# A recurrent layer stack in 279 steps: tile kinds grouped on TensorE, the residual added head by head, growth logarithms kept in the down bank

## The reference, cut to what matters

```python
for l in range(L):                                       # 4 layers
    x = x + _slstm_layer(_ln(x, ln1_w[l]), ...)          # convolution over 4 tokens, gates, recurrence, norm per head
    x = x + _ffn(_ln(x, ln2_w[l]), ff_up[l], ff_down[l]) # gelu(x@up_g) * (x@up_v) @ down, 256 -> 2*336 -> 256
...
def step(carry, wx_t):                                   # 256 steps in order, batch 32, 4 heads of 64
    h, c, n, m = carry
    raw = wx_t + jnp.einsum('bhd,hdgo->bhgo', h, rk) + b
    ir, fr, zr, og = (raw[:, :, 0], raw[:, :, 1], raw[:, :, 2], raw[:, :, 3])
    lfm = m + jax.nn.log_sigmoid(fr)
    mn = jnp.maximum(ir, lfm)
    ig = jnp.exp(ir - mn)
    fg = jnp.exp(lfm - mn)
    cn = fg * c + ig * jnp.tanh(zr)
    nn = fg * n + ig
    hn = jax.nn.sigmoid(og) * cn / nn
    return ((hn, cn, nn, mn), hn)
```

## Time and profile before

| | us |
|---|---|
| median of 3 runs | 3738.53 (3736.28 to 3739.94) |
| the profiled execution, its own time | 3732.63 |
| its span | 3730.9 |
| PE busy | 3615.0 (97%) |
| DVE busy | 3460.5 (93%) |
| ACT busy | 3064.7 (82%) |
| POOL busy | 2253.7 (60%) |

### The profile page before, as it was taken

One profiled execution on the slowest core, in us unless ns is written; L12 is line 12 of the kernel. 1 busy time (PEld: TensorE's weight loads), 2 busy tenths in 40 slices (PEclk: granted clock), 3 DMA queues, 4 the chain that ended last, 5 costly groups with the idle time before them and its releaser, 6 DMA issues. The chain is left out here.

```text
span 3730.9 us, 167466 instructions
## 1 busy us (share of the span) xinstructions
PE 3615.0 (97%) x71481; PEld 2282.1 (61%) x71481; DVE 3460.5 (93%) x9241; ACT 3064.7 (82%) x6357; POOL 2253.7 (60%) x2395
## 2 busy tenths in 40 slices
PE   6999999999999999999999987999999999999997
PEld 3666666665666666666666654666666666666664
DVE  8999999999999999999999987889988898888886
ACT  4999999999999999999999984677776677777675
POOL 3777777777777777777777764444444444444442
PEclk9999999999999999999999998999999999999998
DMA  2000221000000000000000000000000000100000
GB/s 82 25 25 25 56 59 53 25 25 25 25 25 25 25 25 25 25 25 25 25 25 25 25 26 18 24 24 24 24 24 24 24 24 28 32 24 24 24 16 10
DMA packets 99973, 104.27 MB, mean 28 GB/s; under 512 B 17297, under 2 KB 95005, under 8 KB 98729
## 3 DMA queue, kind: packets, MB, share of 16 engines
q1 hardware_dynamic: 99224, 93.56, 8.7%
HBM read 48.52 MB, written 17.53 MB: 18 GB/s over the span
## 5 line engine op out<-in xcount | busy, mean ns | idle before, releaser
L565 POOL TENSOR_TENSOR conv_products<-normed_features,conv_taps_by_token 128x256 f32<-128x256 f32 (+1 forms) x837 | 757.9, 919 | 530.2 <-ACT normed_features L348 530.1
L771 POOL TENSOR_TENSOR exps_of_both_halves<-scores 128x256 f32<-128x256 f32 x512 | 424.2, 851 | 583.8 <-ACT scores L1027 578.4
L295 PE MATMUL banks<-up_centred,after_cell_features 128*32 128x336 f32 x8928 | 740.3, 449 | 1.1 <-ACT after_cell_features L348 0.5
L295 PEld LDWEIGHTS banks<-up_centred,after_cell_features 128*32 128x32 f32 x8928 | 260.5, 109 | 277.6 <-issue 224.1
L302 PE MATMUL banks<-down,hidden_features 112*32 112x256 f32 x6696 | 419.2, 383 | 0.0
L578 POOL TENSOR_TENSOR conv_partial_sums<-conv_products,conv_partial_sums 128x512 f32<-128x512 f32 x279 | 370.5, 1328 | 21.9
L1027 ACT ACTIVATE scores<-scores 128x512 f32<-128x512 f32 x512 | 305.4, 626 | 77.7 <-DVE scores L1175 74.0
L366 ACT ACT_TABLE_LOAD x279 | 358.0, 1283 | 5.2
L381 ACT ACT_TABLE_LOAD x279 | 358.0, 1283 | 5.1
L1175 DVE SCALAR_TENSOR_TENSOR scores<-banks,score_top 128x512 f32<-128x512 f32 x512 | 327.9, 681 | 26.1 <-PE banks L857 25.5
L269 PE MATMUL banks<-recurrent_weights,h_features 64*32 64x256 f32 x8928 | 313.1, 379 | 0.3 <-DVE h_features L509 0.2
(11 more groups left out here) (222 smaller groups left out, 9933.3 us busy)
## 6 DMA issues: line engine op xcount, KB each, us to landing
layer_inputs<-layer_outputs SPq DMA_DIRECT2D x279, 96.0 KB, 2.0
layer_inputs<-in_x SPq DMA_DIRECT2D x280, 32.0 KB, 1.8
x_scratch<-layer_outputs SPq DMA_DIRECT2D x279, 32.0 KB
x_tokens<-in_x SPq DMA_DIRECT2D x32, 256.0 KB, 3.0
context_features<-in_ctx SPq DMA_DIRECT2D x32, 256.0 KB, 3.7
layers_out<-x_scratch SPq DMA_DIRECT2D x32, 256.0 KB, 2.8
out<-result SPq DMA_DIRECT2D x64, 128.0 KB, 1.8
up_centred<-in_ff_up SPq DMA_DIRECT2D x1, 2688.0 KB
```

What stands on the lines that cost most here:

```text
L295: mm = nc.tensor.matmul(bank[group(l), b, 0:UP], xmt[:, n, group(l)], up[:, l, n, at:at + UP], start=n == 0, stop=n == HALF - 1, skip_grou ...
L565: return nc.gpsimd.tensor_tensor(prod[:, i:i + n], xnt[:, j % NRING].rearrange("p n t -> p (n t)")[:, None, :].broadcast_to([P, n, HALF * ...
L771: nc.gpsimd.tensor_tensor(psum[:, i % RING, :], pr[:, i % RING, 0:S], pr[:, i % RING, S:2 * S], ALU.add).then_inc(halves_added, 1)
```

## The change

On PE the order of a step is new: all transposes stand together (`xm`, `xn`, `h`, `hid`), then all products of 64x32 tiles (convolved, recurrent, centred, the bias of the next step, its products of `xnt`), then down, then both up products. On ACT the tanh of z and o open the step, the copies of `ht` (formerly DVE's) and `xnt` stand behind the exponential of the growth, the copy of `xmt` between the exponential and the logarithm of f. The growth logarithm is written into the second half of the bank of the down product, not into the gates; the transposes of `hid` go into the old gate banks. On DVE `yn` is gone: four operations of 128x64, one per head, scale and add the residual at once. `dl` is made at the end of a step, right behind `sf`, and `h`'s second half stands ahead of `hid`. On POOL both 256-wide products come first, then the wide sum, the wide product, and the two other sums, all for the same token.

```diff
+    def hidden_of(j):
+        q = 2 * (j % 2)
+        return bank[0:UT, q:q + 2, :].rearrange("p r (n h t) -> p (r n) h t", n=HALF, h=2)[:, 0:UTILES, 1, :]
...
             for j in range(STEPS):
-                reach(pe, xm_done, j)
                 transposes(CV, D, xm[:, (j - 1) % MRING], xmt_ready)
                 transposes(CV, 0, xn, xnt_ready)
-                add_bias(j)
-                by_head(j, wg, xnt[:, (j - 1) % NRING], 2, GATES)
-                pe.wait_ge(xmt_copied, j + 1)
-                feed_up(UPG, 0).then_inc(g_done, 1)
                 pe.wait_ge(h_done, HALF * (j + 1))
                 transposes(FD, D, h, ht_ready)
-                pe.wait_ge(xnt_copied, j + 1)
-                hidden_features().then_inc(hidt_ready, 1)
+                pe.wait_ge(hid_done, j + 1)
+                hidden_features(j - 1).then_inc(hidt_ready, 1)
                 pe.wait_ge(xs_done, j + 1)
                 by_head(j, wg, xst, 0, 2)
                 pe.wait_ge(ht_copied, j + 1)
                 by_head(j, rk, ht, 0, GATES).then_inc(rec_done, 1)
                 centred().then_inc(cen_ready, 1)
+                pe.wait_ge(ls_done, j + 1)
+                add_bias(j + 1)
+                pe.wait_ge(xnt_copied, j + 1)
+                by_head(j + 1, wg, xnt[:, j % NRING], 2, GATES)
                 pe.wait_ge(hidt_copied, j + 1)
+                pe.wait_ge(grown, j + 1)
                 feed_down().then_inc(down_done, 1)
-                pe.wait_ge(yn_done, j + 1)
+                pe.wait_ge(xmt_copied, j + 1)
+                pe.wait_ge(xm_done, j + 1)
+                feed_up(UPG, 0).then_inc(g_done, 1)
                 feed_up(UPV, UP).then_inc(up_done, 1)
...
+                nc.scalar.activation(gate(j - 1, 2), gate(j - 1, 2), ACT.Tanh).then_inc(z_done, 1)
+                nc.scalar.activation(gate(j - 1, 3), gate(j - 1, 3), ACT.Tanh, scale=0.5).then_inc(o_done, 1)
+                reach(act, d_ready, j)
                 nc.scalar.activation(td[:], dl[:], ACT.Tanh, scale=-0.5).then_inc(td_done, 1)
...
-                copy(both(xmt[:]), bank[:, CV, D:]).then_inc(xmt_copied, 1)
-                copy(both(xnt[:, j % NRING]), bank[:, CV, 0:D]).then_inc(xnt_copied, 1)
...
+                act.wait_ge(ht_ready, j + 1)
+                copy(both(ht[:]), bank[:, FD, D:], 1.0 / H_SCALE).then_inc(ht_copied, 1)
+                copy(both(xnt[:, j % NRING]), bank[:, CV, 0:D]).then_inc(xnt_copied, 1)
                 act.wait_ge(growth_exp, j + 1)
-                act.wait_ge(h_done, HALF * (j + 1))
-                nc.scalar.activation(gate(j - 1, 1), heads(spb[:]), ACT.Ln, bias=1.0).then_inc(growth_log, 1)
+                act.wait_ge(ht_copied, j + 1)
+                nc.scalar.activation(bank[:, FD, D:], spb[:], ACT.Ln, bias=1.0).then_inc(growth_log, 1)
...
                 nc.scalar.activation(heads(fb[:]), gate(j, 1), ACT.Exp).then_inc(f_exp, 1)
+                copy(both(xmt[:]), bank[:, CV, D:]).then_inc(xmt_copied, 1)
                 act.wait_ge(f_exp, j + 1)
                 nc.scalar.activation(fb[:], fb[:], ACT.Ln, bias=1.0).then_inc(f_log, 1)
...
-                nc.vector.tensor_tensor(yn[:].rearrange("p (r n d) -> p r n d", r=2, n=HALF),
...
+                for r in range(2):
+                    for n in range(HALF):
+                        at = slice(r * P + n * DH, r * P + n * DH + DH)
+                        add = nc.vector.scalar_tensor_tensor(out=xm[:, j % MRING, at], in0=bank[:, UPG + r, UP + n * DH:UP + n * DH + DH],
+                                                             scalar=rs[:, 2 * n + r:2 * n + r + 1], in1=xr[:, (j - 3) % XRING, at],
+                                                             op0=ALU.mult, op1=ALU.add)
+                add.then_inc(xm_done, 1)
...
-                reach(pool, taps_rest, j)
-                nc.gpsimd.tensor_tensor(new[:, 3], prod[:, 3], new[:, 4], ALU.add).then_inc(sum3_done, 1)
                 reach(pool, xnt_copied, j)
                 reach(pool, conv_done, j)
+                products(0, 1, j - 1).then_inc(taps_first, 1)
                 products(1, 1, j - 1).then_inc(taps_second, 1)
-                products(0, 1, j - 1).then_inc(taps_first, 1)
-                pool.wait_ge(taps_first, j + 1)
                 reach(pool, sum2_done, j)
+                pool.wait_ge(taps_second, j + 1)
                 nc.gpsimd.tensor_tensor(new[:, 0:2], prod[:, 0:2], old[:, 1:3], ALU.add).then_inc(conv_done, 1)
+                products(2, 2, j - 1).then_inc(taps_rest, 1)
+                pool.wait_ge(taps_rest, j + 1)
+                nc.gpsimd.tensor_tensor(new[:, 3], prod[:, 3], new[:, 4], ALU.add).then_inc(sum3_done, 1)
                 nc.gpsimd.tensor_tensor(new[:, 2], prod[:, 2], old[:, 3], ALU.add).then_inc(sum2_done, 1)
-                pool.wait_ge(xnt_copied, j + 1)
-                pool.wait_ge(sum2_done, j + 1)
-                products(2, 2, j).then_inc(taps_rest, 1)
```

More of the change, by code:

```diff
@@ L346, in _, with copy @@
         def _(act):
-            def copy(dst, src):
-                return nc.scalar.activation(dst, src, ACT.Copy)
+            def copy(dst, src, scale=1.0):
+                return nc.scalar.activation(dst, src, ACT.Copy, scale=scale)
             def both(ap):
@@ L381, in _ @@
                 nc.scalar.preload_act_table(ACT.Gelu)
-                act.wait_ge(sf_done, j + 1)
-                nc.scalar.activation(gate(j, 3), gate(j, 3), ACT.Tanh, scale=0.5).then_inc(o_done, 1)
-                nc.scalar.activation(gate(j, 2), gate(j, 2), ACT.Tanh).then_inc(z_done, 1)
-            act.wait_ge(z_done, STEPS)
+            act.wait_ge(f_log, STEPS)
         @block.vector
@@ L390, in _ @@
             for buf, val in ((xr, 0.0), (h, 0.0), (half_r, 0.0), (ls, NEVER), (dl, 0.0), (xm, 0.0), (xst, 0.0), (prod, 0.0), (hid, 0.0),
-                             (hidt, 0.0), (xnt, 0.0), (xmt, 0.0), (gl, 0.0), (xn, 0.0), (v, 0.0), (sf, 0.0), (rstd, 0.0), (eps, EPS), (bias, 0.0), (pick16, 0.0),
+                             (hidt, 0.0), (xnt, 0.0), (xmt, 0.0), (gl, 0.0), (xn, 0.0), (stat2, 0.0), (rstd, 0.0), (eps, EPS), (bias, 0.0), (pick16, 0.0),
                              (mean_w, 1.0 / D), (begun, 0.25 * H_SCALE), (never, 0.0)):
@@ L399, in _ @@
                 n += 2
+            nc.vector.bn_stats(stat2[:], xm[:, 0]).then_inc(w_step, 1)
+            n += 1
             dve.wait_ge(w_step, n)
@@ L538, in _ @@
                                                op1=ALU.max).then_inc(sf_done, 1)
-                dve.wait_ge(yn_done, j + 1)
-                nc.vector.tensor_tensor(xm[:, j % MRING], yn[:], xr[:, (j - 3) % XRING, :], ALU.add).then_inc(xm_done, 1)
+                dve.wait_ge(sf_done, j + 1)
+                dve.wait_ge(v_done, j + 1)
+                nc.vector.scalar_tensor_tensor(out=dl[:], in0=v[:], scalar=-60.0, in1=sf[:], op0=ALU.max,
+                                               op1=ALU.subtract).then_inc(d_ready, 1)
                 dve.wait_ge(down_done, j + 1)
```

60 lines of the change are left out of this document (26 added, 34 removed).

## The result

The changed kernel takes 3807.64 us (median of 4 runs, 3805.31 to 3809.13), the kernel before 3737.69 on the same chip (4 runs). The ratio is 1.0186, with a 95% interval of 1.0168 to 1.0204: 70 us slower. The forecast was 3760, with 3684 to 3791 as its range. The direction was right and the size was not.

A forecast was written before the change was run, and what follows sets the result against it. PE was taken to set the 7.75 us step, ACT close behind. After the change the loop of POOL's wide product, `dl` and ACT, 4.38 + 3.45 = 7.83, adds 22 us over 279 steps to 3738.5: 3760, range 3684 to 3791.

The forecast's parts named there:

- The loop of the wide product, `dl` and ACT: `dl` ends 0.28 after POOL's wide product, ACT then copies `xnt`: 4.38 + 3.45 = 7.83 us a step, 22 us more; chance 0.64.
- the spacings of "0.30" and their neighbours: Three unknown ACT spacings in the loop, to tanh, gelu and exponential, each put at 0.30 us, between 0.28 and 0.32.
- 7.73 to 7.94: Range of the loop's step in us, from three spacings of 0.28 to 0.32 and one of 0 to 0.09.
- PE alone would need 7.42: Grouping PE's products by tile kind saves 0.33 us a step, leaving PE 7.42 of its own.
- the seven and in the four: PE's changes of tile kind a step, seven before and four after, at 0.11 us each.
- not 0.7 to 0.8: Sign in the changed profile: the `dl` row on VectorE grows from 0.49 to 0.7 or 0.8 us.
- The recurrence at 7.58: Path of the recurrence through all engines, a sum of spacings: 7.58 us a step, below the loop's 7.83.
- `dl` does meet POOL: Against the free-port rival: `dl` meets no POOL instruction, the recurrence decides at 7.58, 47 us less, 3691; chance 0.22.
- restart whole: Rival: `dl` restarts whole after POOL's instruction, 0.13 us more a step, 7.96, total 3797 us; chance 0.05.
- misses its gap: Rival: `xn` comes after POOL's wide sum has begun, 1.03 us more a step, some 4050 us; chance 0.04.
- faster: Outcome faster than before, by the free port or PE's own pace (3646 to 3671 us): chance 0.24.
- slower: Outcome slower than before, by the rest of the loop's case and the two rivals above it: chance 0.66.

The follow-up runs named there:

- e14: Changed kernel with `sf` written into the PSUM bank of the transposes, and PE's bias and normed products of the next step behind both up products: 3684.4 us, ratio 0.9853.
- e9: Changed kernel with `sf` in the PSUM bank and PE's down products between the centred products and the next step's bias: 3734.8 us, ratio 0.9997.
- e1: Changed kernel, but POOL's wide product waits until `dl` has ended: 3749.3 us, ratio 1.0039.
- e3: Changed kernel, but POOL's wide product of 128x512 is split into two products of 128x256 in the same place: 3751.0 us, ratio 1.0038.
- e8: Changed kernel with POOL's order untouched, but `sf` written into the PSUM bank of the transposes, so `dl` reads one operand from PSUM: 3739.0 us, ratio 1.0009.
- e5: One of the nine kernels with runs of 96 short products; the text does not tell what it changed or its time.
- e4: Kernel before with only POOL's loop taken from the changed kernel: 3809.5 us, ratio 1.0204.
- e7: Changed kernel with POOL's order of before put back: 3847.7 us, ratio 1.0291.

## Why the prediction was right or wrong

- **The loop of the wide product, `dl` and ACT decides: right.** `td` waits 0.25 a step, `xst` fell to 0.41, PE waits for `h` and `hid` (31.9 + 23.5 us in 100 steps, 0.55 a step; 0.4 forecast), and the three experiments that free `dl` remove the loss of the loop.
- **Its size: too small.** Two terms: the wide sum starts 1.57 after the first product and not 1.50, which had been read in the old loop of POOL (what makes the 0.07 is not shown); and the spacings of "0.30" and their neighbours came out 0.02 longer in all. 7.92 lies inside the 7.73 to 7.94 that the unknown spacings allowed, by luck, since the one that grew was not among them; it gave 44 us instead of 22, which alone would have stayed in the range.
- **"PE alone would need 7.42": the step that failed.** Its arithmetic held: with one dear change of tile kind more, PE needs 7.53 in e14. (It counted down to up as a change, in the seven and in the four alike; by the 1.32 against the 1.43 of e9 it costs none of the 0.11.) But the step counted a long run of short products as a pure gain and put its price at nothing. The run has one: 38 pauses, and 26 us with the loop as it is, which put the time outside the range. No row of the kernel before shows such a pause; its longest run was 96 products.
- **`dl` took 0.92, not 0.7 to 0.8.** It came at 3.43 after the copy and not 3.7 (in part because the four pieces of `xm` take 0.77 together, 0.84 was put down). Its end, which POOL sets, came at 4.44, so an earlier start only made it longer.
- **The recurrence at 7.58: a little too long.** e14, with the same recurrence, shows that it is at most 7.53 (`h`'s second half starts 0.30 behind the first in e14, 0.34 was put down); the many steps of 7.57 and 7.58 in e1, e3 and e8 do not confirm the sum.
- **The rivals.** `dl` does meet POOL (in 276 of 279 steps). It does not restart whole: it ends 0.27 behind POOL, not 0.41, and no run shows the 0.13 more that this rival was added up from. `xn` misses its gap only in single steps (it takes over 0.9 in one step of the changed kernel, and in 14 of e9).
- **The chances do not sum as said.** By its own terms, faster has 0.22 + 0.05 = 0.27 and not 0.24, slower 0.54 + 0.04 + 0.05 = 0.63 and not 0.66.

## What to carry to other kernels

Look for the last instruction that two engines' loops have in common, and check what runs beside it: a change of order on an engine far from the bound (POOL, 57% busy) cost 76 us by itself. Moving one operand of the waiting instruction into PSUM ended the wait without a change of POOL's order (`dl` from 919 to 421 ns, e8). And a group of short instructions made longer saved switches, but 136 of them with their weight loads brought 38 pauses of PE, 22 us: look for idle time with no releaser in the group behind such a one.

## What the runs showed of the hardware

- PE stood still, with 0.34 to 1.35 us from one start to the next, in down or in the normed products, 256 instructions or a multiple of it apart, when 136 short products with their weight loads stood in one run of some 2.6 us; with runs of 96 it did so once in nine kernels (e5). In all 187 pauses of this study it went on 1.1 to 1.6 us after the end of the last packet of the instruction queue. That the supply of instructions is late there follows from this, from the place and from the two-way test; no row names it as the releaser. One such packet came for every 256 of PE's instructions (562 for 144,020).
- A VectorE instruction with two inputs in SBUF that meets one of POOL's ended 0.27 to 0.28 us behind that one (`xst`, `dl`, and `xm` in e4), `xn` 0.15 to 0.16, in the steps shown here; `dl` with one input in PSUM took 421 ns beside POOL's wide product (e8). POOL's next instruction was not held up by the wait: it began 0.08 after the last one's end in e7.
